# A sorted mixture of experts: b3 folded into centred weights, the gate weight into the silu*g product, and the result halves summed by VectorE

## The reference

```python
x = x + _L0_conv_ref(_ln_c(x), ...)     # q, k, v projections, softmax over the 256 tokens of an image
t = _to_tokens(x)                       # 4096 tokens of 128
t = t + _L0_ffn_ref(_ln_t(t), Wg, W1, W2, W3, b3)

# _L0_ffn_ref
logits = jnp.einsum('bsd,de->bse', x, Wg)
top_logits, top_idx = jax.lax.top_k(logits, 2)
top_w = jax.nn.softmax(top_logits, axis=-1)      # C: these weights at the chosen experts
h = jnp.einsum('bsd,edf->bsef', x, W1)           # f = 384
g = jnp.einsum('bsd,edf->bsef', x, W3) + b3
act = jax.nn.silu(h) * g
out = jnp.einsum('bse,bsef,efd->bsd', C, act, W2)
```

## Time and profile before

| | us |
|---|---|
| median of 3 runs | 348.44 (347.86 to 348.78) |
| span of the profiled execution | 344.9 |
| front, to the end of the last scatter of rows | 0 to 144.5 |
| expert stage, to the start of the last scatter of results | 146.1 to 326.7 |

### The profile page before, as it was taken

The page is one execution under the profiler, slowest core; times in us unless marked ns, Lnnn a source line. Parts: engine busy times, 40 slices in busy tenths (PEclk is TensorE's granted clock), DMA queues, the critical chain, the costliest instruction groups (busy, mean ns, idle before and its releaser), DMA issues.

```text
span 344.9 us, 7790 instructions
## 1 busy us (share of the span) xinstructions
PE 267.4 (78%) x1723; PEld 217.8 (63%) x1724; DVE 235.2 (68%) x768; ACT 180.1 (52%) x442; POOL 199.0 (58%) x243
## 2 busy tenths in 40 slices
PE   1997986786977940769898999999999979989200
PEld 0454654554644520259898989999898979888100
DVE  2356787887686358028686887888787858768733
ACT  1445663763661331027676776767676757766100
POOL 6222158778788777504656666666666566666700
PEclk9999899999897695869999999999999999999655
DMA  3996301101111112220122221221221212122678
GB/s 115 324 312 204 99 26 39 55 31 39 46 41 39 46 40 83 81 58 27 49 59 59 54 61 51 57 61 46 61 60 47 61 46 61 47 64 84 221 220 275
DMA packets 31812, 29.76 MB, mean 86 GB/s; under 512 B 4992, under 2 KB 29504, under 8 KB 31664
## 3 DMA queue, kind: packets, MB, share of 16 engines
q1 hardware_dynamic: 24704, 18.38, 18.7%
q0 software_dynamic: 4320, 8.92, 7.7%
q10 hardware_dynamic: 2768, 2.23, 1.9%
HBM read 17.51 MB, written 12.01 MB: 86 GB/s over the span
## 4 chain that ended last, share of the span: by engine, by line
POOL 24%; PE 21%; issue 19%; DMA 14%; DVE 9%; SPq 7%; ACT 4%; POOLq 1%; DVEq 1%; ACTq 0%
POOL result_rows L1172 10%; POOL w_all L1169 6%; POOL sorted_rows L1140 6%; DMA result_rows<-w_all,xs 4%; DMA xs<-sorted_rows 3%; PE bank L641 3%; DMA w_all<-result_rows 3%; DMA x_all<-x_dram 3%; PE bank L659 3%; SPq L403 3%; PE bank L642 3%; PE bank L643 3%; PE bank L649 2%; ACT row_buf L736 2%; PE bank L575 2%
## 5 line engine op out<-in xcount | busy, mean ns | idle before, releaser
L1172 POOL DMA_INDIRECT result_rows<-w_all,xs x71 | 71.9, 1013 | 59.3 <-POOL w_all L1169 57.1
L1140 POOL DMA_INDIRECT sorted_rows<-row_buf,position x64 | 65.2, 1019 | 22.7 <-issue 19.3
L575 PE MATMUL bank<-all_ones 128*128 128x512 bf16 x205 | 63.4, 420 | 13.0 <-DMA bkv<-L_conv_bv_dram 7.6
L641 PE MATMUL bank<-w_up,xs_hi 128*128 x142 | 55.1, 388 | 6.9 <-issue 6.9
L659 PE MATMUL bank<-w_down,act_hi 128*128 x213 | 58.9, 345 | 0.8 <-ACT y_parts L815 0.8
L1063 DVE TENSOR_TENSOR gate<-bank,b_all 128x384 f32<-128x384 f32 x71 | 39.6, 558 | 28.6 <-PE bank L643 27.8
L810 ACT ACTIVATE act_hi<-bank 128x384 fp32r<-128x384 f32 x71 | 35.0, 493 | 26.8 <-PE bank L649 26.4
L643 PE MATMUL bank<-w_up,xs_hi 128*128 x142 | 48.8, 343 | 0.0
L642 PE MATMUL bank<-w_up,xs_lo 128*128 x142 | 48.7, 343 | 0.0
L661 PE MATMUL bank<-w_down,act_lo 128*128 x213 | 47.6, 223 | 0.0
L1071 DVE TENSOR_TENSOR act_rows<-silu_h,gate 128x384 f32<-128x384 f32 x71 | 43.3, 610 | 3.1
(11 more groups left out here) (134 smaller groups left out, 436.9 us busy)
## 6 DMA issues: line engine op xcount, KB each, us to landing
xs<-sorted_rows SPq DMA_DIRECT2D x71, 65.0 KB
w_all<-result_rows SPq DMA_DIRECT2D x16, 256.0 KB, 4.2
w_all<-L_ffn_W_dram SPq DMA_DIRECT2D x2, 1536.0 KB, 8.8
x_all<-x_dram SPq DMA_DIRECT2D x8, 256.0 KB, 3.8
out_dram<-w_all ACTq DMA_DIRECT2D x8, 256.0 KB, 4.1
w_all<-L_ffn_W_dram SPq DMA_DIRECT2D x3, 512.0 KB, 11.2
b_all<-L_ffn_b_dram SPq DMA_DIRECT2D x1, 1536.0 KB, 10.8
result_rows<-w_all,xs POOLq DMA_INDIRECT x71, 2.3
```

The source lines that it names most:

```text
L575: nc.tensor.matmul(bank[free_bank][:].rearrange("p (a b) -> p a b", a=4), all_ones[:], all_ones[:].unsqueeze(1).broadcast_to([P, 4, P]), s ...
L641: nc.tensor.matmul(o, xs_hi[s.par][:], w[0], start=True, stop=False)
L1140: nc.gpsimd.indirect_dma_start(out=sorted_rows.ap(), out_offset=bass.IndirectOffsetOnAxis(ap=position[u.par][:, c:c + 1], axis=0), in_=row ...
L1172: nc.gpsimd.indirect_dma_start(out=result_rows.ap(), out_offset=bass.IndirectOffsetOnAxis(ap=xs[s.ring][:].bitcast(I32)[:, DEST:DEST + 1], ...
```

## The change

What it computes instead: with m the column means of W, a row x of sum zero, and 1 added to each of its 128 channels, (x + 1)(W - m + b3/128) = xW + b3. So W1 and W3 are centred by a matmul with I - 1/128, b3/128 is added to W3 by a matmul with one row, both in the front, and the transposed rows get 1 added as they are rounded. The gate weight, which multiplied the result, now multiplies silu(h)*g. The halves of the result are summed out of PSUM by one `tensor_reduce` on DVE; POOL only scatters. Fillers per iteration go from 17 to 12 and write bank 0; `rank` writes bank 6; bank 7 holds the centred weights.

Its core (semaphore declarations, shapes of the unchanged down split and the constants on POOL are cut):

```diff
@@ SP @@
             for u in range(1, 4):
                 load_x(Step(0, u))
+            sp.dma_start(b3_row[:].rearrange("p e f -> p (e f)"),
+                         b3.rearrange("e f -> (e f)").unsqueeze(0)).then_inc(b3_in, 16)
             sp.dma_start(w_all[:, :, 0, :], W1.rearrange("e c f -> c e f")).then_inc(expert_in, 16)
...
-            sp.dma_start(b3_all[:].rearrange("p e f -> p (e f)"),
-                         b3.rearrange("e f -> (e f)").partition_broadcast(P)).then_inc(b3_in, 16)
@@ PE, front @@
+            def center_up(u, j):
...
+                at_least(pe, up_lo_ready, u.n * 2 + j)
+                o = bank[7][:, 0:F]
+                up_w = w_all[:, ds(u.n, 1), j, :].rearrange("p a f -> p (a f)")
+                last = nc.tensor.matmul(o, center[:], up_w, start=True, stop=(j == 0))
+                if j == 1:
+                    last = nc.tensor.matmul(o, ones_row[:], b3_row[:, ds(u.n, 1), :].rearrange("p a f -> p (a f)"),
+                                            start=False, stop=True)
+                last.then_inc(centered_ps, 1)
             def iteration(i):
-                keep_busy(7, 3)
+                keep_busy(3)
                 if exists(new):
                     transpose_xn(new)
-                keep_busy(7, 1)
+                if exists(old):
+                    center_up(old, 0)
                 if exists(i):
                     transpose_probs(i)
-                keep_busy(7, 1)
                 if exists(i.shift(-2)):
                     rank(i.shift(-2))
-                keep_busy(6, 1)
                 if exists(new):
                     project_kv(new)
...
-                keep_busy(6, 3)
+                keep_busy(2)
                 if exists(old):
                     transpose_tn(old)
-                keep_busy(6, 1)
+                keep_busy(1)
                 if exists(i):
                     attend(i)
-                keep_busy(6, 3)
+                if exists(old):
+                    center_up(old, 1)
+                keep_busy(2)
                 if exists(old):
                     route(old)
@@ ACT, front @@
                 if exists(old):
                     normalise_tiles(old, [TPU - 1])
+                if exists(old):
+                    round_up_weights(old, 0)
...
                 if exists(old):
                     copy_tnt(old)
+                    round_up_weights(old, 1)
                 if exists(i.shift(2)) and not first:
                     normalise_x(i.shift(2))
                 if exists(i):
-                    round_weights(i)
+                    round_down_weights(i)
@@ DVE, front @@
                 if exists(old):
-                    split_up_weights(old)
+                    split_down_weights(old)
                 if exists(i):
                     add_mix_bias(i)
                 if exists(old):
-                    split_down_weights(old)
+                    split_up_weights(old, 0)
...
                 if exists(old):
                     choose(old)
+                    split_up_weights(old, 1)
                 if exists(i.shift(2)):
                     add_br(i.shift(2))
@@ ACT, expert stage @@
-                nc.scalar.activation(xs_hi[s.par][:], bank[0][:, 0:P], ACT.Copy).then_inc(xs_hi_ready, 1)
+                nc.scalar.activation(xs_hi[s.par][:], bank[0][:, 0:P], ACT.Copy, bias=1.0).then_inc(xs_hi_ready, 1)
...
-                if s.has(-2):
-                    scale_result(s.shift(-2))
@@ DVE, expert stage @@
             def gated(s):
-                dve.wait_ge(gate_ready, s.n + 1)
+                dve.wait_ge(g_ps, s.n + 1)
                 dve.wait_ge(silu_ready, s.n + 1)
                 at_least(dve, actt_ps, s.n - 1)
-                nc.vector.tensor_tensor(act_rows[s.par][:], silu_h[s.par][:], gate[s.par][:],
-                                        ALU.mult).then_inc(act_ready, 1)
+                nc.vector.scalar_tensor_tensor(out=act_rows[s.par][:], in0=bank[3 + s.par][:, 0:F],
+                                               scalar=xs[s.ring][:, WEIGHT:WEIGHT + 1], in1=silu_h[s.par][:],
+                                               op0=ALU.mult, op1=ALU.mult).then_inc(act_ready, 1)
...
+            def sum_result(s):
+                dve.wait_ge(y_ps, s.n + 1)
+                at_least(dve, y_out[s.ring], s.round * 16)
+                nc.vector.tensor_reduce(ys[s.ring][:], bank[7][:, 0:2 * C].rearrange("p (a c) -> p c a", a=2),
+                                        AX.X, ALU.add).then_inc(y_sb, 1)
             def step(s):
-                if s.has(0):
-                    if s.ring == 0:
-                        load_experts(s, dve_experts, mybir.EngineType.DVE)
+                if s.has(-3):
+                    sum_result(s.shift(-3))
                 if s.has(1):
                     split_rows(s.shift(1))
                 if s.has(0):
-                    add_b3(s, dve_experts[s.offset])
                     gated(s)
                 if s.has(-1):
                     split_act(s.shift(-1))
@@ POOL, expert stage @@
             def scatter_results(s):
-                pool.wait_ge(y_sb, s.n + 1)
-
-                at_least(pool, y_out[s.ring], s.round * 16)
-                nc.gpsimd.tensor_tensor(ys[s.ring][:], y_parts[s.par][:, 0, :], y_parts[s.par][:, 1, :],
-                                        ALU.add).then_inc(y_sum, 1)
-                wait_in_front(pool, waited_pool, (y_sum, s.n + 1))
+                wait_in_front(pool, waited_pool, (y_sb, s.n + 1))
```

More of the change, by code:

```diff
@@ L213, in build @@
         silu_h = [sb(f"silu_h{i}", [P, F]) for i in range(2)]
-        gate = [sb(f"gate{i}", [P, F]) for i in range(2)]
         act_rows = [sb(f"act_rows{i}", [P, F]) for i in range(2)]
@@ L224, in build @@
         assert NU * K * UC + RING * P <= E * 3 * F
-        y_parts = [sb(f"y_parts{i}", [P, 2, C]) for i in range(2)]
         pool_consts = sem("pool_consts")
@@ L235, in build @@
         w_lo_ready = sem("w_lo_ready")
+        centered_ps = sem("centered_ps")
+        up_hi_ready = sem("up_hi_ready")
+        up_lo_ready = sem("up_lo_ready")
         wq_t_ps = sem("wq_t_ps")
@@ L360, in run_units, with run_slots @@
                 iteration(Step(0, i))
-        def run_slots(eng, step, before=None):
+        def run_slots(eng, step, before=None, behind=2):
             if before is not None:
@@ L371, in run_slots @@
                     step(Slot(q, o, RING, NS))
-            for n in range(rounds * RING, NS + 2):
+            for n in range(rounds * RING, NS + behind):
                 step(Slot(0, n, RING, NS))
@@ L810, in copy_act_t @@
                 nc.scalar.activation(act_hi[s.par][:], bank[5 + s.par][:, 0:F], ACT.Copy).then_inc(act_hi_ready, 1)
-            def scale_result(s):
-                act.wait_ge(y_ps, s.n + 1)
-                at_least(act, y_sum, s.n - 1)
-                nc.scalar.activation(y_parts[s.par][:].rearrange("p a c -> p (a c)"),
-                                     bank[7][:, 0:2 * C], ACT.Copy,
-                                     scale=xs[s.ring][:, WEIGHT:WEIGHT + 1]).then_inc(y_sb, 1)
             def step(s):
@@ L825, in step @@
                     copy_act_t(s.shift(-1))
-                if s.has(-2):
-                    scale_result(s.shift(-2))
-            run_slots(act, step, copy_rows_t)
+            run_slots(act, step, copy_rows_t, behind=1)
             def store(u):
@@ L977, in weigh_and_place @@
                 dve.wait_ge(rank_ps, u.n + 1)
-                after(nc.vector.tensor_tensor(place[:], bank[7][:, 0:TPU * E].rearrange("p (t e) -> p t e", e=E),
+                after(nc.vector.tensor_tensor(place[:],
+                                              bank[6][:, RANK:RANK + TPU * E].rearrange("p (t e) -> p t e", e=E),
                                               region[:].unsqueeze(1).broadcast_to([P, TPU, E]), ALU.add),
@@ L1076, in split_rows @@
                 at_least(dve, g_ps, s.n - 1)
-                nc.vector.tensor_tensor(xs_lo[s.par][:], bank[0][:, 0:P], xs_hi[s.par][:].bitcast(F32),
-                                        ALU.subtract).then_inc(xs_lo_ready, 1)
+                nc.vector.scalar_tensor_tensor(out=xs_lo[s.par][:], in0=bank[0][:, 0:P], scalar=1.0,
+                                               in1=xs_hi[s.par][:].bitcast(F32), op0=ALU.add,
+                                               op1=ALU.subtract).then_inc(xs_lo_ready, 1)
             def split_act(s):
@@ L1098, in step @@
                     split_act(s.shift(-1))
-            run_slots(dve, step, split_rows)
+            run_slots(dve, step, split_rows, behind=3)
             def add_half(u, k, done):
```

63 lines of the change are left out of this document (33 added, 30 removed).

## The result

The change is slower. Its median is 354.04 us (349.45 to 359.69, 13 runs), that of the kernel before in the same session 348.44 us (346.34 to 353.37, 13 runs); the ratio is 1.0114, 95% interval 1.0081 to 1.0148. Forecast were 341.4 us and a range up to 347.2. The profiled execution has a span of 356.9 us at a mean granted clock of 0.866. That is above its median: other executions of this kernel have spans from 347.7 us at 0.908 to 357.9 at 0.866, so I take mechanisms and waits from the profile and totals from the medians.

The account below looks back on a forecast made before the run. PE and POOL were taken to bound the expert stage, POOL and the chain to `seen` alternately the front. Front +1.7, stalls -5.0, tail -3.7 made -7.0 on 344.9, so 337.9; plus 3.5, 341.4 us, range 336.8 to 347.2.

Parts of the forecast that it names:

- Reduction: Expert stage, DVE: summing the result halves from PSUM by `tensor_reduce` takes 421 ns, between 220 and 688.
- tail: End of expert stage: last scatter starts 1.3 us after the last matmul instead of 5.0, gain 3.7 us.
- Ring stalls: Expert stage: row tile loads wait for the scatter eight slots back; 5.0 of 5.5 us of stalls regained.
- the ring case: Rival, expert stage: the eight-slot loop stays binding, stalls move to DVE's wait, only the end gains; 346.4 us, chance 0.10.
- Together 0.2 per unit: Front, ACT: split rounding ahead of the exponentials and `normalise_x` behind the second centring add 0.2 us per unit.
- The chain grows by 0.75 per unit: Front: the ACT, PE and DVE chain ending in `seen` lengthens 0.75 us per unit, bounds 0.5 and 1.3.
- a gain of 0.5 us: Front's start: without the 1.5 MB b3 load and five fillers, first work comes 0.5 us earlier, bounds 0 and 1.1.
- signs of failure: Front: first `xs` load later than 152 us, or granted clock under 0.8 in its windows, means the forecast failed there.
- The 0.25 that shows of `route`: Front, PE: +0.95 us ahead of `route`, most hidden by 0.7 us before its reader; 0.25 shows.
- a front that is wholly hidden: Rival: POOL's block absorbs the longer front chain entirely and stalls go; -9.2 us or so, 339.0 us, chance 0.18.
- I count half: Front: POOL's block takes turns with the chain, so half its growth shows: six units x 0.75 / 2 = 2.2 us.
- The slower rival: Front: with 12 fillers PE's clock stays at 1.2 GHz, centring pair 3.1 us instead of 1.56; 351.7 us, chance 0.09.

Follow-up runs that it names:

- e1: Kernel before's front with the change's expert stage, b3 not added: 339.71 us, ratio 0.9712 to the kernel before.
- e6: The change with only the first centring product moved, behind `project_kv`, 12 fillers: 341.97 us, ratio 0.9815 to the kernel before.
- e13: e12 plus one PE wait for VectorE's `member` ahead of `transpose_probs`, no instruction added, third chip: 375.56 us, ratio 1.0165 to the kernel before.
- e15: The change itself, rerun on a third chip: 383.24 us, ratio 1.035 to the kernel before there.
- e12: The kernel of e5, rerun on a third chip: 367.68 us, ratio 0.9968 to the kernel before there.
- e3: The change with 17 fillers per unit in place of 12: 350.32 us, ratio 0.9997 to the kernel before.
- e2: The kernel before with 12 fillers per unit in place of 17, nothing else: 346.88 us, ratio 0.9921 to the kernel before.
- e14: e12 with 12 fillers, three fewer, on the third chip: 368.97 us, ratio 1.0004 to the kernel before there.
- e5: The change with both centring products where PE waited for `xk`, the second in bank 6, 15 fillers: 336.52 us, ratio 0.9681 to the kernel before.
- e4: The change with its float32 centring products replaced by bf16 fillers into bank 7, same waits: 346.62 us, ratio 0.9901 to the kernel before.
- e8: The change without the one-row float32 product that adds b3: 350.79 us, ratio 1.0029 to the kernel before.
- e11: e6 with ACT's `normalise_x` ahead of the second rounding, on another chip: 372.08 us, ratio 1.005 to the kernel before there.

## Why the prediction was wrong

**Reduction, tail, POOL: right.** 416 ns against 421, 1.28 us against 1.3, 2.16 us a slot against 2.16. Worked out were 8.7 us for stage and tail; the profile shows 10.2, and e1, which has nothing else, 10 of the median. The gated product was mis-sized by 60 ns (618 against 558); VectorE had the room. Ring stalls: L646 waited 4.4 us for `xs`, 2.0 of them ahead of the first slot, so 2.4 in the ring, under the 3 that would have been the ring case.

**The front: the step that failed** is the sum of the queue places, "Together 0.2 per unit" and, after it, "The chain grows by 0.75 per unit". It priced each moved instruction where it stands, and for the first centring product it priced nothing but its length. What it left out is the condition under which that product may start: bank 7 is single, so product 0 of one unit waits for the split of product 1 of the unit before, and that split is the one of which the prediction itself says that it "stands behind `choose`". For `down` and its bank 7 the prediction did ask who waits for the bank; in the front it did not. Measured: 1.1 us of waiting and 0.9 of product ahead of `transpose_probs`, 6.3 us of waits of PE and 10.9 of DVE in six units, and 1.5 us a pass where 0.75 / 2 was counted (1.0 to 1.2 of it at the full clock). Moving that one product gave back 10 of the 14 us (e6). How much of that is the wait and how much the product, e13 was to say and doesn't.

**The first pass failed too.** There the prediction counted a gain of 0.5 us. ACT's first normalisation did come 0.3 earlier (32.64 against 32.98), but the first block came 6.6 us later, at half the clock. Chance is in this number: e1, with the front of before, has its first block at 48.73, 2.0 us behind before's; the change on the third chip (e15) has it at 54.20, e12 at 46.91. The prediction's own signs of failure both showed: a first `xs` load at 168.54 against a limit of 152, and a clock of 0.50 and 0.76 against 0.8.

**Two sums.** The 0.25 that shows of `route` is not in the chain's 0.75, which is 0.2 + 0.55; with it the chain is 1.0, inside the bounds. And a front that is wholly hidden comes to 348.4 - 9.2 = 339.2, not 339.0.

**"I count half"** failed with it. POOL's block hides a chain that is now and then shorter than it. Once the chain is longer in every unit, all of it shows: idle times of 1.9 to 2.9 us ahead of the blocks at 96.04 and 110.89.

**The slower rival** gave 351.7 us, near the 354.04 measured, and the clock did fall in the front. Its mechanism, 12 fillers in place of 17, is a part: in the change five fillers more bring back 4 of the 14 us (e3), while in the other orders they are worth nothing or less (e2, e14), though the clock is lower with 12 there too (0.883 against 0.907, 0.881 against 0.896). The clock also goes with the order: 0.896 in e12, 0.885 in e13 and 0.848 in the change beside them (e15, medians), and e5 with all float32 products has 1.00 up to 105 us. Its sentence that the centrings "themselves are work for PE" was right only where they fill a gap, as in e5. Its price of the pair at 1.2 GHz, 3.1 us, was close: the profile has 1.65 and 1.64 at 39.73 and 41.31 us. At the full clock a product shows as 0.91, and its successor starts 0.84 later (115.22, 116.06), where the sum had 0.78.

**The rule of the Trainium skill** in "TensorE: Matmul & The Clock Gate", HAM oscillation, is that gaps in PE's work bring the clock down. The first pass of the change agrees: 3.80 us of waiting, then 1.2 GHz up to about 52 us. The advice in "VectorE: DVE Perf Modes", Rules for kernel authors, against the reduction does not decide here, since it costs 416 ns beside a 2.16 us slot of PE.

**What stays open**: how the 14 us split between the loop and the lower clock. The profile gives 7.7 of its 22.3 us to the five passes with the loop and the rest to the two ends, where the granted clock is 0.50, but it is one execution, 4.6 us above the median span. Whether the waits bring the clock down is not shown, and e4 (float32 products out: half), e6 (first product moved: 10 us) and e8 (b3's product out: 3 us) overlap. Whether the second rounding ahead of `normalise_x` costs anything was not settled by e11. And e5's 3.2% over the kernel before is that of one chip; on another (e12) the two can't be told apart, while against the change it is some 4% on both (1.0114 - 0.9681, 1.035 - 0.9968).

## What to carry to other kernels

For every instruction that a change puts into a queue, write down what it waits for as well as how long it takes, the release of its buffer above all; with a single buffer, its producer's next turn waits for the last reader of the turn before, and then for all that this reader stands behind. Then follow what is queued behind it on its own engine until you come back to the engine that was waited for: here such a loop through three queues cost 1.0 to 1.2 us in a pass at the full clock, and nothing hid it. Look at the first pass by itself, where other waits and another clock hold. Put extra work where its engine waits anyway, and give both halves a buffer of their own.

## What the runs showed of the hardware

- The time of one kernel follows PE's granted clock run by run: spans of the change from 347.7 us at 0.908 to 357.9 at 0.866. Between kernels it need not: e2 is 0.8% faster than before at 0.883 against 0.907.
- A gated product that reads PSUM, SBUF and a scalar per partition takes 618 ns for 384 elements, an addition of PSUM and SBUF 558.
- Chips differ in the front and not in the expert stage (one profiled execution each). From the first to the last result scatter e12 takes 348.04 - 188.72 = 159.3 us, and the same kernel as e5 took 318.01 - 159.90 = 158.1. Blocks of row scatters start 100.27 - 81.80 = 18.5 us apart in e12 and 97.44 - 84.93 = 12.5 in e5. In e12 VectorE and ScalarE both stand still for nearly 4 us in one pass, and go on together; "remote" says that no instruction and no DMA of the core's profile was found as the releaser:

```profile
93.41 0.69 DVE L949 TENSOR_TENSOR x_all<-bank,x_all 128x512 f32 x1 [3.82 <-remote]
93.48 0.60 ACT L733 ACTIVATE xn_t<-bank 128x512 f32<-128x512 f32 x1 [3.79 <-remote]
```

What that is the runs don't tell, nor whether it is all of the difference. A gain in the front measured on one chip was not the gain on another.
